# Key side of a four-layer kernel: gathers and projections paired across slots, copies ahead of maxima, exponentials two by two

## The chip, the cores and the metric

One core of one Trainium2 chip runs the whole program. The metric is the device time in microseconds (us) of one execution.

## What is computed

The reference adds four layers to `x` (32 batches of 64 rows by 512, float32), with a context tensor of the same shape: a cross-attention over 8 heads, a feed-forward with quantized weights, a linear cross-attention, and a projection with a low-rank mixture of experts. The change lies in the part that prepares the third layer from the context. Cut to that part, the reference is:

```python
kh = jnp.einsum('bcn,oc->bon', k, Wk).reshape(b, HEADS, DIM_HEAD, -1)   # k = v = ctx, n = 512
vh = jnp.einsum('bcn,oc->bon', v, Wv).reshape(b, HEADS, DIM_HEAD, -1)
kh = jax.nn.softmax(kh, axis=-1)
context = jnp.einsum('bhdn,bhen->bhde', kh, vh)
```

`context` is 64 by 64 for each head and batch. The kernel keeps, as `k.M`, that product already multiplied by the output weights `Wo`.

## The kernel before

`key_side` (from L214) is the first stage of the program. Behind it come `attention0`, `feed_forward`, `query_side` and `projection_and_experts`, and each stage ends in a meeting of all engines. The key side works on 16 tiles; tile t is two batches, 128 rows of the context. Each engine has its program written out by hand, as a loop over t and over four slots c of a tile, and semaphores join them. In slot (t, c) tile t is turned and gathered, while the next tile, t+1, is projected. These are the pieces, by the names of the helpers:

- `keys(t, c)` (L610, TensorE, "K"): one 128-wide chunk of the key projection, three float16 passes of two matmuls each, into `psK[c % 2]`. It waits until the exponentials of chunk c-2 have read that bank (`ek_ok`).
- `keys_max(t, c)` (L408, VectorE): the maximum over the row of `psK`, 1,024 wide, into `mk`.
- `exponentials(t, c)` (L553, ScalarE): two exponentials of 512 from `psK` into `ek`, each with its sum.
- `turn(t, j, b)` (L621, TensorE, "T"): four transposes of `ek` into `psT[b]`. ScalarE (L586, b = 0) or VectorE (`turned`, L413, b = 1, and b = 0 as well for j = 3) copies the bank to `eT`.
- `gather(t, j)` (L631, TensorE, "G"): `eT` times the turned context `cT`, summed over j = 0 to 3 in the single bank `psG`. Since the first gather of a tile starts a new sum there, it waits until the sum of the tile before has been copied away.
- That copy is the one to `gT` (L592, ScalarE), once a tile, in slot c = 0; `matrix(t)` (L644, TensorE, "M") multiplies `gT` by the weights in slot 2 of the tile after, and VectorE's `matrix` (L423) scales the result into `k.M`.
- `context(t)` (L602, TensorE, "C"): four transposes of the next context tile into `psM`, copied to `cT` by ScalarE (`transposed`, L548).

The two waits of a gather that the change touches stand in three lines:

```python
if j == 0:
    pe.wait_ge(cT_ok, t + 1)
    wait(pe, gT_ok, t)
```

Between these, VectorE also has sums of magnitudes of the feed-forward's weights (`magnitudes`, L429, slot 3 of tiles 0 to 4), row statistics (`stats`, L436, slots 0 and 3 of tiles 6 to 13) and, in the last tile, the reciprocal deviations (`vec_x`, from L98). ScalarE has two sums of magnitudes a tile in slots 2 and 3 of tiles 0 to 4, and one in tile 5. GpSimd casts the feed-forward's weights from tile 7 on (`ternary`, L366), behind `scales` (L469) on VectorE in slot 0 of tile 7.

Of the kernel before, what the change touches and what calls it, by code (L numbers as in the profile page):

```python
# [30 lines left out]
NC = L // P  # L31
BATCHES = 32
TILES = BATCHES * D // P
# [180 lines left out]
def key_side(nc, a, k):  # L214

    with ExitStack() as ctx:
# [41 lines left out]
        def sums_at(t):  # L258
            return range(3 * t, min(3 * t + 3, UNITS))
# [142 lines left out]
        def _(dve):  # L402
# [5 lines left out]
            def keys_max(t, c):  # L408
                dve.wait_ge(k_ps, NC * t + c + 1)
                wait(dve, ek_ok, 2 * NC * (t - 1) + 2 * c + 2)  # L410
                dve.tensor_reduce(mk[:, c, :], psK[c % 2][:, :, :], X, ALU.max, negate=True).then_inc(mk_ok, 1)  # L411

            def turned(t, j, b):  # L413
                dve.wait_ge(t_ps, 2 * NC * t + 2 * j + b + 1)
                wait(dve, g_ps, NC * (t - 1) + j + 1)
                dve.tensor_copy(eT[b][:, j, :], psT[b][:, :]).then_inc(eT_dve, 1)  # L416
# [97 lines left out]
            keys_max(1, 0)  # L514
            for t in range(TILES + 1):
                for c in range(NC):
                    if t + 1 + (c + 1) // NC < TILES:
                        keys_max(t + 1 + (c + 1) // NC, (c + 1) % NC)
                    if t < TILES:
                        if c == NC - 1:  # L520
                            turned(t, c, 0)
                        turned(t, c, 1)
                    if c == 0 and t < TILES:
                        sums(t)
                    if c == 0 and 1 <= t < 4:
                        biases(t - 1)
                    if c == 1 and t + 2 < TILES:
                        low(t + 2)
                    if c == 2 and t > 0:
                        matrix(t - 1)  # L530
                    if c == 3:
                        for u in sums_at(t):
                            if u % 3 == 2:
                                magnitudes(u)
                    if c == 0 and t == CAST - 1:
                        dve.wait_ge(wa_act, UNITS - UNITS // 3)
                        dve.wait_ge(wa_dve, UNITS // 3)
                        dve.tensor_reduce(asum[:, :], k.wabs[:, :, :], X, ALU.add).then_inc(sum_ok, 1)
                    if c == 0 and t == CAST:
                        scales()  # L540
                    if c in (0, 3) and STATS <= t < STATS + TILES // 2:
                        stats(2 * (t - STATS) + c // 3)
                    if c == 1 and t == TILES - 1:
                        vec_x(dve)

        @block.scalar
        def _(act):
# [33 lines left out]
            for t in range(TILES + 1):  # L581
                for c in range(NC):
                    if t < TILES and c < NC - 1:
                        act.wait_ge(t_ps, 2 * NC * t + 2 * c + 1)
                        wait(act, g_ps, NC * (t - 1) + c + 1)
                        act.activation(eT[0][:, c, :], psT[0][:, :], ACT.Copy).then_inc(eT_act, 1)  # L586
                    if t + 1 + (c + 1) // NC < TILES:
                        exponentials(t + 1 + (c + 1) // NC, (c + 1) % NC)
                    if c == 0 and t > 0:
                        act.wait_ge(g_ps, NC * t)  # L590
                        wait(act, m_ps, t - 1)
                        act.activation(gT[:, :], psG[:, :], ACT.Copy).then_inc(gT_ok, 1)  # L592
                    if c == 1 and t + 1 < TILES:
                        transposed(t + 1)
                    if c >= 2 and c - 2 < len(sums_at(t)):
                        magnitudes(sums_at(t)[c - 2])
                    if c == 1 and t == TILES - 1:
                        act_x(act)

        @block.tensor  # L600
        def _(pe):
# [97 lines left out]
            pe.wait_ge(w_ok, VO_OK)  # L699
            for t in range(TILES + 1):  # L700
                for c in range(NC):
                    if t + 1 + (c + 1) // NC < TILES:
                        keys(t + 1 + (c + 1) // NC, (c + 1) % NC)
                    if t < TILES:
                        turn(t, c, 0)
                        turn(t, c, 1)
                    if c > 0 and t < TILES:
                        gather(t, c - 1)
                    if c == 0 and t > 0:
                        gather(t - 1, NC - 1)  # L710
                    if c == 1 and t + 1 < TILES:
                        if t == CAST:
                            pe.wait_ge(inv_ok, 1)
                        context(t + 1)
                    if c == 2 and t > 0:
                        matrix(t - 1)
                    if c == 3 and t == CAST - 1:
                        pe.wait_ge(sum_ok, 1)
                        pe.wait_ge(M_ok, t)
                        pe.matmul(psM[:, 0:3], k.ones32[:, :], asum[:, :], start=True, stop=True).then_inc(sum_ps, 1)  # L720
# [1136 lines left out]
```

## Time and profile before

| | |
|---|---|
| median of 3 runs | 778.26 us (777.91 to 778.72) |
| the profiled execution | 775.0 us, its span 773.2 us |
| granted clock of TensorE, mean over the span | 0.96 of full speed |
| TensorE busy | 684.9 us, 89% |
| VectorE busy | 624.1 us, 81% |
| ScalarE busy | 487.6 us, 63% |
| GpSimd busy | 382.3 us, 49% |
| the key side | from 0 to about 221.6 us of the span |

The span runs from the first to the last instruction. The execution's own time is 1.8 us more. Shares of busy time are averages over five stages; only the first is changed. In a timeline the ends of matmuls are modelled, and one group of matmuls overlaps the next, so that the pace of TensorE is read from one start to the next start. An "idle before" is counted from a modelled end.

### The profile page before, as it was taken

The numbers are of one execution on the slowest core, as the hardware profiler recorded it, in microseconds if no ns is written. First come the engines' busy times: TensorE is split into PE (matmuls) and PEld (weight loads), VectorE is DVE, ScalarE is ACT, GpSimd is POOL, SyncE is SP. The second block draws the span as 40 slices with busy tenths as digits, with TensorE's granted clock in tenths as the row PEclk, the third lists the DMA queues.
The fourth block names the chain that finished last, engine by engine and source line by source line (L and its number), as shares of the span: only waits on it lengthen the run. The fifth ranks groups of instructions, "written<-read, shape, count | busy, mean of one in ns | idle before, by whom it ended". The sixth has DMA issues, their size and how long they took to land. (4 is left out here: it accounts for less than half of the span.)

```text
span 773.2 us, 17952 instructions
## 1 busy us (share of the span) xinstructions
PE 684.9 (89%) x6761; PEld 355.1 (46%) x6761; DVE 624.1 (81%) x1001; ACT 487.6 (63%) x896; POOL 382.3 (49%) x281
## 2 busy tenths in 40 slices
PE   4999999999977777399999859999999999938998
PEld 2455455554545555144444314444444444415743
DVE  6888788888636677589999658999999999939675
ACT  4878876767526667277766416878878788744320
POOL 2000029999915665021221127768677686728730
PEclk9999999999989999599999969999999999977999
DMA  6244546556352331033344300000000000007505
GB/s 166 80 136 163 172 151 178 147 128 169 79 136 72 79 86 32 14 59 60 70 77 78 57 0 1 1 2 1 1 2 1 1 2 1 1 1 117 104 27 191
DMA packets 94185, 54.93 MB, mean 71 GB/s; under 512 B 78548, under 2 KB 78548, under 8 KB 94100
## 3 DMA queue, kind: packets, MB, share of 16 engines
q1 hardware_dynamic: 93348, 53.25, 27.1%
q8 instruction: 55, 0.90, 0.5%
q10 hardware_dynamic: 752, 0.52, 0.3%
q14 instruction: 30, 0.25, 0.1%
HBM read 32.20 MB, written 4.19 MB: 47 GB/s over the span
## 5 line engine op out<-in xcount | busy, mean ns | idle before, releaser
L1312 POOL TENSOR_TENSOR query_qn<-query_eq,query_rq 128x1024 f32<-128x1024 f32 x64 | 121.7, 1902 | 56.9 <-DVE query_rq L1246 55.1
L558 ACT ACTIVATE keys_ek<-keys_psK,keys_mk 128x512 f32<-128x512 f32 x128 | 86.8, 683 | 38.4 <-DVE keys_mk L411 36.6
L411 DVE TENSOR_REDUCE keys_mk<-keys_psK 128x2 f32<-128x1024 f32 x64 | 77.8, 1217 | 17.1 <-PE keys_psK L617 16.9
L1237 DVE TENSOR_REDUCE query_mq<-query_psQ 128x16 bf16<-128x1024 f32 x64 | 75.6, 1181 | 5.3 <-PE query_psQ L1380 5.0
L1321 ACT ACTIVATE query_eq<-query_psQ 128x1024 f32<-128x1024 f32 x64 | 65.1, 1018 | 22.6 <-PE query_psQ L1393 22.6
L1243 DVE TENSOR_REDUCE query_lq<-query_eq 128x16 f32<-128x1024 f32 x64 | 77.2, 1207 | 2.6 <-ACT query_eq L1321 2.5
L1040 POOL TENSOR_SCALAR ff_hr<-ff_h,ff_qs 128x1376 f32<-128x1376 f32 x16 | 22.6, 1412 | 104.5 <-DVE ff_qs L1087 104.5
L1402 PE MATMUL query_psX<-all_ident,query_qn 128*128 128x128 f32 x512 | 70.7, 282 | 0.0
L628 PE MATMUL keys_psT<-all_ident,keys_ek 128*128 128x128 f32 x512 | 70.0, 280 | 0.0
L640 PE MATMUL keys_psG<-keys_eT,keys_cT 128*64 128x512 f32 x256 | 69.0, 617 | 1.0 <-issue 0.9
L628 PEld LDWEIGHTS keys_psT<-all_ident,keys_ek 128*128 128x128 f32 x512 | 54.8, 141 | 27.8 <-issue 20.0
L1328 ACT ACTIVATE query_qT<-query_psX 128x1024 f32<-128x1024 f32 x64 | 65.4, 1022 | 1.2 <-PE query_psX L1402 1.2
L1412 PE MATMUL query_psF<-query_qT,all_M 128*64 128x512 f32 x256 | 61.8, 604 | 1.1 <-ACT query_qT L1328 1.1
L1402 PEld LDWEIGHTS query_psX<-all_ident,query_qn 128*128 128x128 f32 x512 | 55.5, 142 | 15.7 <-issue 14.3
L376 POOL TENSOR_SCALAR keys_st<-all_ring 128x1024 bf16<-128x1024 f32 (+2 forms) x16 | 60.7, 3795 | 1.3
L364 POOL TENSOR_SCALAR keys_cs_hi<-all_cf 128x512 f16<-128x512 f32 x16 | 9.9, 618 | 95.5 <-DMA all_cf<-in_ctx_dram 87.0
L1161 PE MATMUL ff_psG<-all_wgT,ff_xT 128*128 128x512 bf16 (+1 forms) x192 | 46.8, 367 | 10.2 <-DMA ff_xT<-ff_xq 10.2
L416 DVE COPY keys_eT<-keys_psT 128x512 f32<-128x512 f32 x80 | 53.1, 680 | 2.4 <-PE keys_psT L628 2.3
L1134 ACT ACTIVATE ff_r<-ff_psG,all_sg 128x512 f32<-128x512 f32 (+1 forms) x48 | 30.8, 642 | 36.3 <-PE ff_psG L1161 34.7
L1166 PE MATMUL ff_psU<-all_wuT,ff_xT 128*128 128x512 bf16 (+1 forms) x192 | 46.1, 363 | 0.0
L1175 PE MATMUL ff_psD<-all_wdT,ff_hT 128*128 128x512 bf16 (+1 forms) x176 | 42.1, 390 | 4.4 <-DMA ff_hT<-ff_hq 4.4
L586 ACT ACTIVATE keys_eT<-keys_psT 128x512 f32<-128x512 f32 x48 | 28.7, 598 | 19.2 <-PE keys_psT L628 19.0
(255 smaller groups left out, 1481.9 us busy)
## 6 DMA issues: line engine op xcount, KB each, us to landing
all_ring<-in_L_ffn_w_down_dram SPq DMA_DIRECT2D x8, 688.0 KB, 4.3
all_ring<-in_L_ffn_w_gate_dram SPq DMA_DIRECT2D x10, 512.0 KB, 4.5
all_ring<-in_L_ffn_w_up_dram SPq DMA_DIRECT2D x10, 512.0 KB, 3.8
all_x_res<-in_x_dram SPq DMA_DIRECT2D x4, 1024.0 KB, 6.2
att_ctx_n<-in_ctx_dram SPq DMA_DIRECT2D x16, 256.0 KB, 3.0
out_dram<-all_x_res SPq DMA_DIRECT2D x16, 256.0 KB, 2.2
all_cf<-in_ctx_dram SPq DMA_DIRECT2D x15, 256.0 KB, 2.7
att_w_nat<-in_L_ffn_W_dram SPq DMA_DIRECT2D x4, 256.0 KB, 4.2
```

The source lines that it names most:

```text
L376: pool.tensor_scalar(st[v % 2][:, 0:w], r, -ROUND, 0.0, ALU.add, ALU.add).then_inc(cast_ok, 1)
L411: dve.tensor_reduce(mk[:, c, :], psK[c % 2][:, :, :], X, ALU.max, negate=True).then_inc(mk_ok, 1)
L558: act.activation(ek[t % 2][b][:, c, :], psK[c % 2][:, b, :], ACT.Exp, bias=mk[:, c, b:b + 1], accum_out=le[t % 2][:, b, c:c + 1]).then_inc ...
L628: mm = pe.transpose(chunk(psT[b], c), chunk(ek[t % 2][b][:, c, :], j), k.ident[:, :])
L640: mm = pe.matmul(psG[HALF[b], :], cT[t % 2][:, j, b * D:(b + 1) * D], eT[b][:, j, :], start=j == 0, stop=j == NC - 1)
L1237: dve.tensor_reduce(mq[g % 2][:, :, 0:HEADS], psQ[g % 2][:, :, :].rearrange("p b (h d) -> p b h d", d=D), X, ALU.max, negate=True).then_in ...
L1243: dve.tensor_reduce(lq[:, :], eq[g % 3][:, :, :], X, ALU.add).then_inc(lq_ok, 1)
L1312: pool.tensor_tensor(qn[m % 2][:, :, :], eq[m % 3][:, :, :], rq[m % 2][:, :].unsqueeze(2).broadcast_to([P, 2 * HEADS, D]), ALU.mult).then_ ...
L1321: act.activation(eq[g % 3][:, :, :].rearrange("p h d -> p (h d)"), psQ[g % 2][:, :, :].rearrange("p b n -> p (b n)"), ACT.Exp).then_inc(eq ...
L1328: act.activation(qT[t % 2][:, :, c * P:(c + 1) * P], psX[:, :, :].rearrange("p b (j n) -> p (b j) n", n=P), ACT.Copy).then_inc(qT_ok, 1)
L1402: mm = pe.transpose(psX[:, b, j * P:(j + 1) * P], qn[g % 2][:, b * HEADS + 2 * j:b * HEADS + 2 * j + 2, :].rearrange("p h d -> p (h d)"), ...
L1412: mm = pe.matmul(psF[HALF[b], :], k.M[:, 2 * t + b, j, :], qT[t % 2][:, b * NC + j, :], start=j == 0, stop=j == NC - 1)
```

## The change

On TensorE the pieces of every second slot (c = 1 and 3) are put in reverse. Slots 0 and 2 still run K, T, G; slots 1 and 3 now run G, T, K, so that the K of slot 1 stands beside the K of slot 2, and the G of slot 0 beside the G of slot 1. On VectorE the copies of a slot go ahead of its maximum. On ScalarE slots 0 and 2 have both pairs of exponentials, slots 1 and 3 none.

```diff
--- before.py
+++ after.py
@@ -514,12 +514,12 @@
             keys_max(1, 0)
             for t in range(TILES + 1):
                 for c in range(NC):
-                    if t + 1 + (c + 1) // NC < TILES:
-                        keys_max(t + 1 + (c + 1) // NC, (c + 1) % NC)
                     if t < TILES:
                         if c == NC - 1:
                             turned(t, c, 0)
                         turned(t, c, 1)
+                    if t + 1 + (c + 1) // NC < TILES:
+                        keys_max(t + 1 + (c + 1) // NC, (c + 1) % NC)
                     if c == 0 and t < TILES:
                         sums(t)
                     if c == 0 and 1 <= t < 4:
@@ -584,7 +584,9 @@
                         act.wait_ge(t_ps, 2 * NC * t + 2 * c + 1)
                         wait(act, g_ps, NC * (t - 1) + c + 1)
                         act.activation(eT[0][:, c, :], psT[0][:, :], ACT.Copy).then_inc(eT_act, 1)
-                    if t + 1 + (c + 1) // NC < TILES:
+                    if c % 2 == 0 and (t > 0 or c > 0) and t + (c + NC) // NC < TILES:
+                        exponentials(t + (c + NC) // NC, c)
+                    if c % 2 == 0 and t + 1 + (c + 1) // NC < TILES:
                         exponentials(t + 1 + (c + 1) // NC, (c + 1) % NC)
                     if c == 0 and t > 0:
                         act.wait_ge(g_ps, NC * t)
@@ -699,19 +701,23 @@
             pe.wait_ge(w_ok, VO_OK)
             for t in range(TILES + 1):
                 for c in range(NC):
-                    if t + 1 + (c + 1) // NC < TILES:
+                    if c % 2 == 1 and t < TILES:
+                        gather(t, c - 1)
+                    if c % 2 == 0 and t + 1 + (c + 1) // NC < TILES:
                         keys(t + 1 + (c + 1) // NC, (c + 1) % NC)
                     if t < TILES:
                         turn(t, c, 0)
                         turn(t, c, 1)
-                    if c > 0 and t < TILES:
-                        gather(t, c - 1)
-                    if c == 0 and t > 0:
-                        gather(t - 1, NC - 1)
                     if c == 1 and t + 1 < TILES:
                         if t == CAST:
                             pe.wait_ge(inv_ok, 1)
                         context(t + 1)
+                    if c % 2 == 1 and t + 1 + (c + 1) // NC < TILES:
+                        keys(t + 1 + (c + 1) // NC, (c + 1) % NC)
+                    if c == 2 and t < TILES:
+                        gather(t, c - 1)
+                    if c == 0 and t > 0:
+                        gather(t - 1, NC - 1)
                     if c == 2 and t > 0:
                         matrix(t - 1)
                     if c == 3 and t == CAST - 1:
```

The first place is TensorE at the start of a tile, tile 2 being turned and tile 3 projected. L617 is K, L628 is T, L640 is G, L607 is C; a last digit in a name is the number of a buffer. Before:

```order
L640 MATMUL keys_psG<-keys_eT0,keys_cT1 64x512 [waits keys_eT_dve]
L640 MATMUL keys_psG<-keys_eT1,keys_cT1 64x512
L617 MATMUL keys_psK0<-keys_cs_hi1,all_wk_hi 128x512 [waits keys_ek_ok,keys_lo_ok]
L617 MATMUL keys_psK0<-keys_cs_hi1,all_wk_hi 128x512
L617 MATMUL keys_psK0<-keys_cs_lo1,all_wk_hi 128x512 x2
L617 MATMUL keys_psK0<-keys_cs_hi1,all_wk_lo 128x512 x2
L628 MATMUL keys_psT0<-all_ident,keys_ek00 128x128 [waits keys_eT_act,keys_ek_ok]
L628 MATMUL keys_psT0<-all_ident,keys_ek00 128x128 x3
L628 MATMUL keys_psT1<-all_ident,keys_ek01 128x128 [waits keys_eT_dve,keys_ek_ok]
L628 MATMUL keys_psT1<-all_ident,keys_ek01 128x128 x3
L640 MATMUL keys_psG<-keys_eT0,keys_cT0 64x512 [waits keys_eT_act,keys_eT_dve,keys_gT_ok,keys_cT_ok]
L640 MATMUL keys_psG<-keys_eT1,keys_cT0 64x512
```

Now (two lines further down in the file, as L619, L630, L642 and L609):

```order
L630 MATMUL keys_psT1<-all_ident,keys_ek01 128x128 [waits keys_eT_dve,keys_ek_ok]
L630 MATMUL keys_psT1<-all_ident,keys_ek01 128x128 x3
L642 MATMUL keys_psG<-keys_eT0,keys_cT1 64x512 [waits keys_eT_dve]
L642 MATMUL keys_psG<-keys_eT1,keys_cT1 64x512
L642 MATMUL keys_psG<-keys_eT0,keys_cT0 64x512 [waits keys_eT_act,keys_eT_dve,keys_gT_ok,keys_cT_ok]
L642 MATMUL keys_psG<-keys_eT1,keys_cT0 64x512
L630 MATMUL keys_psT0<-all_ident,keys_ek00 128x128 [waits keys_eT_act,keys_ek_ok]
L630 MATMUL keys_psT0<-all_ident,keys_ek00 128x128 x3
L630 MATMUL keys_psT1<-all_ident,keys_ek01 128x128 [waits keys_eT_dve,keys_ek_ok]
L630 MATMUL keys_psT1<-all_ident,keys_ek01 128x128 x3
L609 MATMUL keys_psM<-all_ident,all_cf1 128x128 [waits keys_M_ok,keys_lo_ok]
L609 MATMUL keys_psM<-all_ident,all_cf1 128x128 x3
```

The two gathers into `psG` now stand one behind the other, the last of the tile before and the first of the new one, and the second of them has the wait on `gT_ok`. Before, a K and a T with a place of their own stood between them.

The second place is ScalarE in slots 0 and 1 of the same tile. L586 is the copy of a turned bank, L558 the exponentials, L592 (now L594) the copy to `gT`, L551 the copy of the turned context. Before:

```order
L586 ACTIVATE keys_eT0<-keys_psT0 128x512 [waits keys_g_ps,keys_t_ps]
L558 ACTIVATE keys_ek10,keys_le1<-keys_psK1,keys_mk 128x512 [waits keys_rl_ok,keys_t_ps,keys_mk_ok]
L558 ACTIVATE keys_ek11,keys_le1<-keys_psK1,keys_mk 128x512
L592 ACTIVATE keys_gT<-keys_psG 128x512 [waits keys_m_ps,keys_g_ps]
L586 ACTIVATE keys_eT0<-keys_psT0 128x512 [waits keys_g_ps,keys_t_ps]
L558 ACTIVATE keys_ek10,keys_le1<-keys_psK0,keys_mk 128x512 [waits keys_rl_ok,keys_t_ps,keys_mk_ok]
```

Now:

```order
L586 ACTIVATE keys_eT0<-keys_psT0 128x512 [waits keys_g_ps,keys_t_ps]
L558 ACTIVATE keys_ek10,keys_le1<-keys_psK0,keys_mk 128x512 [waits keys_rl_ok,keys_t_ps,keys_mk_ok]
L558 ACTIVATE keys_ek11,keys_le1<-keys_psK0,keys_mk 128x512
L558 ACTIVATE keys_ek10,keys_le1<-keys_psK1,keys_mk 128x512 [waits keys_rl_ok,keys_t_ps,keys_mk_ok]
L558 ACTIVATE keys_ek11,keys_le1<-keys_psK1,keys_mk 128x512
L594 ACTIVATE keys_gT<-keys_psG 128x512 [waits keys_m_ps,keys_g_ps]
L586 ACTIVATE keys_eT0<-keys_psT0 128x512 [waits keys_g_ps,keys_t_ps]
L551 ACTIVATE keys_cT1<-keys_psM 128x512 [waits keys_g_ps,keys_c_ps]
```

Two pairs of exponentials stand between the first copy and the copy to `gT`, where there was one.

The third place is VectorE between slot 3 of tile 2 and slot 0 of tile 3. L416 is a copy of a turned bank, L411 a maximum, L433 a sum of magnitudes. Before:

```order
L411 TENSOR_REDUCE keys_mk<-keys_psK0 128x2
L416 COPY keys_eT0<-keys_psT0 128x512
L416 COPY keys_eT1<-keys_psT1 128x512
L433 TENSOR_REDUCE all_wabs<-all_ring 128x1
L411 TENSOR_REDUCE keys_mk<-keys_psK1 128x2
L416 COPY keys_eT1<-keys_psT1 128x512
```

Now:

```order
L416 COPY keys_eT0<-keys_psT0 128x512
L416 COPY keys_eT1<-keys_psT1 128x512
L411 TENSOR_REDUCE keys_mk<-keys_psK0 128x2
L433 TENSOR_REDUCE all_wabs<-all_ring 128x1
L416 COPY keys_eT1<-keys_psT1 128x512
L411 TENSOR_REDUCE keys_mk<-keys_psK1 128x2
```

The copies of slot 3 moved ahead of its maximum, and so did the copy of slot 0.

## Rows read from the trace of the kernel before

**Rows 1.** the page's 40 slices of 19.3 us: busy tenths of TensorE, its granted clock

```profile
PE   4999999999977777399999859999999999938998
...
PEclk9999999999989999599999969999999999977999
```

**Rows 2.** timeline of TensorE, tiles 6 and 7: start, us from start to end, what ran

```profile
103.77 1.08 PE L640 MATMUL keys_psG<-keys_eT,keys_cT 128*64 128x512 f32 x4
104.68 1.04 PE L649 MATMUL keys_psM<-all_wv_wo,keys_gT 128*64 128x128 f32 x16
105.65 0.39 PE L617 MATMUL keys_psK<-keys_cs_hi,all_wk_hi 64*128 64x512 f16 x2
105.88 0.38 PE L617 MATMUL keys_psK<-keys_cs_lo,all_wk_hi 64*128 64x512 f16 x2
...
106.41 1.09 PE L628 MATMUL keys_psT<-all_ident,keys_ek 128*128 128x128 f32 x8
107.43 1.08 PE L640 MATMUL keys_psG<-keys_eT,keys_cT 128*64 128x512 f32 x4
108.44 0.39 PE L720 MATMUL keys_psM<-keys_asum,all_ones 128*128 128x3 f32 x2
...
114.33 0.66 PE L607 MATMUL keys_psM<-all_ident,all_cf 128*128 128x128 f32 x4
114.91 0.39 PE L617 MATMUL keys_psK<-keys_cs_hi,all_wk_hi 64*128 64x512 f16 x2
```

**Rows 3.** TensorE's gathers: their group on the page, timeline at two late ones

```profile
L640 PE MATMUL keys_psG<-keys_eT,keys_cT 128*64 128x512 f32 x256 | 69.0, 617 | 1.0 <-issue 0.9
...
60.66 1.09 PE L628 MATMUL keys_psT<-all_ident,keys_ek 128*128 128x128 f32 x8
61.95 1.08 PE L640 MATMUL keys_psG<-keys_eT,keys_cT 128*64 128x512 f32 x4 [0.19 <-issue]
...
87.79 1.08 PE L640 MATMUL keys_psG<-keys_eT,keys_cT 128*64 128x512 f32 x4 [0.56 <-issue]
```

**Rows 4.** timeline of ScalarE ahead of those gathers, and after one maximum

```profile
59.92 0.69 ACT L558 ACTIVATE keys_ek<-keys_psK,keys_mk 128x512 f32<-128x512 f32 x1 [0.48 <-DVE keys_mk L411]
...
61.26 0.59 ACT L592 ACTIVATE keys_gT<-keys_psG 128x512 f32<-128x512 f32 x1
...
87.10 0.59 ACT L592 ACTIVATE keys_gT<-keys_psG 128x512 f32<-128x512 f32 x1
...
107.78 0.69 ACT L558 ACTIVATE keys_ek<-keys_psK,keys_mk 128x512 f32<-128x512 f32 x1 [2.21 <-DVE keys_mk L411]
```

**Rows 5.** timeline of VectorE, tiles 6 and 7

```profile
106.52 1.22 DVE L411 TENSOR_REDUCE keys_mk<-keys_psK 128x2 f32<-128x1024 f32 x1
107.66 1.28 DVE L416 COPY keys_eT<-keys_psT 128x512 f32<-128x512 f32 x2
108.85 0.68 DVE L440 BATCH_NORM_STATS2 keys_six<-all_x_res 128x6 f32<-128x512 f32 x1
...
109.67 1.21 DVE L411 TENSOR_REDUCE keys_mk<-keys_psK 128x2 f32<-128x1024 f32 x1
```

**Rows 6.** groups by line, 20 to 215 us: VectorE's five magnitudes (busy, mean ns)

```profile
L433 DVE TENSOR_REDUCE all_wabs<-all_ring 128x1 f32<-128x1024 f32 (+2 forms) x5 | 5.3, 1068 | 0.0
```

**Rows 7.** timeline of VectorE in the last tile of the key side

```profile
212.02 0.69 DVE L416 COPY keys_eT<-keys_psT 128x512 f32<-128x512 f32 x1 [1.23 <-PE keys_psT L628]
...
215.31 0.69 DVE L416 COPY keys_eT<-keys_psT 128x512 f32<-128x512 f32 x1
```

**Rows 8.** TensorE by stretch: us, PE busy, ..., granted clock before the DMA share

```profile
239.90:242.00 2.10, 0.05 (x1) 0.00 (x0) 0.73 (x2) 0.93 (x1) 1.25 (x2) 1.00 0.03 6
...
436.10:438.80 2.70, 0.04 (x1) 0.00 (x0) 2.56 (x8) 0.00 (x0) 1.33 (x1) 1.00 0.71 134
438.80:442.20 3.40, 3.02 (x8) 1.09 (x9) 0.18 (x1) 1.44 (x1) 0.08 (x1) 0.50 0.19 38
```

**Rows 9.** timeline of GpSimd: its last cast on the key side

```profile
209.07 4.84 POOL L376 TENSOR_SCALAR keys_st<-all_ring 128x1376 bf16<-128x1376 f32 x1
```

## The prediction

> **What bounds the kernel now.** I read the page's slices first. TensorE is busy without a break in the first eleven slices, at the full clock [rows 1]; that is the key side, the only stage that changes. Then the timeline of TensorE. From start to start, T takes 1.02 us (106.41 to 107.43), G 1.01 (to 108.44), or 0.91 where M follows it, M 0.97, K 0.76, C 0.58 [rows 2]. A tile is four times K, T and G, with one G at 0.91, and M and C: 3.04 + 4.08 + 3.94 + 0.97 + 0.58 = 12.6 us, with nothing waited for. So 16 tiles are about 200 of the 221.6 us of the stage: TensorE is the bound, and both what it saves and what it waits for shows in full.
>
> **What switching costs.** G is 0.10 shorter before M than before a matmul of another shape. G and M use the array as 128x64, T and C as 128x128, K as 64x128; so 0.10 us goes by when the shape changes. C has four transposes and T eight, so that one is (1.02 - 0.58) / 4 = 0.11, and T's remaining 0.14 is 0.10 for the way out and 0.04 for the way in. For G's way in I take the same 0.05. K loses about 0.08 on its way out: the first pass takes 0.23, three would be 0.68. The Trainium skill, in TensorEngine Tiling (Array Packing), section Key Properties, says that changing the tiling mode drains TensorE. The trace agrees, with the 0.10 us.
>
> **The change on TensorE.** Nothing is added or removed; only places move. The new order by slot, without waits:
> - slot 0: K after K 0.75, T 1.02, G before G 0.91: 2.68
> - slot 1: G after G 0.96, T before C 0.93, C 0.53, K before K 0.68: 3.10
> - slot 2: K 0.75, T 1.02, G before M 0.91, M 0.87: 3.55
> - slot 3: G after M 0.96, T 1.02, K before K 0.68: 2.66
>
> That is 12.0 us, 0.6 less than 12.6. If that were all, 15 tiles would save 9 us.
>
> **The wait that it meets.** The gather of slot 1 is the first of its tile. It writes `psG`, and must wait for the copy to `gT`. The trace has this wait already: the copy starts at 61.26 and takes 0.59, and the gather, 0.27 later than its T allows (1.29 behind it, not 1.02), starts at 61.95; the other ends at 87.69, and its gather starts at 87.79 [rows 3, 4]. So a gather starts 0.10 after that copy's end. In all they lost about 1.2 us before: 0.9 of modelled idle time [rows 3], and some 0.1 at each of three. Now this gather stands directly behind the last gather of the tile before, and the copy behind two pairs of exponentials on ScalarE. From the start of slot 0 (its K) the chain is:
> - T starts at 0.75 and ends 1.09 later, 1.84.
> - VectorE's copy starts at 1.88, and its next instruction 0.60 later (two copies in 1.19 [rows 5]), at 2.48. This is the maximum of slot 0's K, which now stands behind the copy. It takes 1.22, to 3.70.
> - The exponentials start 0.04 after a maximum (106.52 + 1.22, then 107.78 [rows 4, 5]), at 3.74. From the first of a pair to the copy to `gT` are 1.34 us (59.92 to 61.26). The copy runs from 5.08 to 5.67.
> - The gather starts at 5.77. TensorE was ready at 2.68: it stands for 3.09 us. After standing, this G takes 1.01 and not 0.96.
>
> A tile takes 12.0 + 3.09 + 0.05 = 15.1, or 2.5 us more than 12.6. It holds for tiles 1 to 14, which turn and project: **+35 us**. Queued behind the gather are the T of slot 1, C and two K, and with them every maximum and exponential of the next tile. Their work is done in the remaining 9.3 us of a tile with time to spare. By the same sums the last pair of exponentials of a tile ends at about 14.1, before slot 0 of the next starts at 15.1 with the K that needs its bank.
>
> **What makes the chain longer.** VectorE takes the maximum of the K before slot 0 at about 0.20, which holds it for 1.14 (106.52 to 107.66), to 1.35; then come statistics (0.82, 108.85 to 109.67 [rows 5]) or magnitudes, and then the copy, which could start at 1.88. The statistics of slot 3 end at 2.17, so the copy starts 0.29 late: 8 tiles, +2.3. Five magnitudes take 1.07 on the mean [rows 6], 0.08 less from start to start, and 0.53 of each is free: +2.3. Taken off are the 1.2 us lost before. ScalarE's magnitudes cost nothing: from its last pair to its next copy it has 2.4 us (14.1 to 16.5), and two of them, each at most two exponentials of 0.69 long, take no more than 2.8; the 0.4 over falls ahead of exponentials that wait for VectorE anyway. Without that cover they would cost up to 1 us in each of five tiles.
>
> **Edges.** In tile 0 there is no copy to wait for, and its first gather waits for a copy of ScalarE about as long as K does now: 0. In the last tile the copy of slot 2 stands 3.29 behind that of slot 1, with the row deviations between [rows 7]. The third gather waits for it, and T, two copies and the last gather now come behind that gather: T and a copy, 1.02 + 0.6, are no longer hidden. The first gather waits 0.9 for the copy to `gT` (0.17 of G's tail, 0.04, 0.59, 0.10). So +2.5, between 0 and 4.
>
> Together 35 + 2.3 + 2.3 - 1.2 + 2.5 = +41 us with the clock as it is.
>
> **The clock.** TensorE now stands still 14 times, for about 2.9 us by modelled ends, 3.2 with statistics and up to 3.9 with magnitudes. Before, a stretch of 2.10 us with 0.05 busy passed at the full 2.4 GHz, and after one of 2.70 with 0.04 busy the granted clock was 0.50, 1.2 GHz, for 3.4 us [rows 8]. The new ones are longer than both. At half the clock TensorE does half the work, and for 9.3 us after each wait it alone sets the pace: a fall costs up to 3.4 / 2 = 1.7 us, 1.6 on the mean, since the end of the wait may lie in it. How many are followed by a fall no row tells: the bounds are 0 and 14, 0 and +24 us. I take 11, nearer to the row of 2.70, since all of them are longer; but one case is little to go by: **+17 us**.
>
> GpSimd's casts end at 213.91 [rows 9], 7.7 us before the stage. They move back with the `scales` of tile 7 by less than the stage's end does, so they bind nothing.
>
> **The sum.** The profiled execution took 775.0; 775.0 + 41 + 17 = 833. The median of the runs is 3.3 us above it, so I forecast 836.
>
> **Rivals.**
> - *The clock holds.* The wait is there, but no fall follows. For it: 2.10 us passed without one. Against it: the row of 2.70. Time 778 + 41 = 819. Chance 0.17.
> - *Falls are worse.* One after each wait, with a second stretch at 1.2 GHz after some, or TensorE still slow in slot 0, where the chain to the copy begins: 35 us or more for the clock, 855. Chance 0.08.
> - *Fewer switches win.* By the rule of the Trainium skill named above this kernel would be faster, since five of thirteen changes of shape in a tile go. As a mechanism of this kernel: 0.6 us saved in each tile, if the gather of slot 1 finds `psG` free. It decides at a wait of 0.6 us a tile; the copy would have to end by 3.2 of the tile's time. That gives 9 us, 769, or a little less, since GpSimd's casts would move up by only 7 x 0.6, to 209.7, with a transfer behind them, and might end the stage: 770. Against it: even with ScalarE idle, the last gather ends at 2.85, and the copy and its two handovers (0.04 + 0.59 + 0.10) bring 3.6. Chance 0.04.
> - *The change doesn't do what it says.* The order of the instructions shows both gathers side by side, and the copy behind two pairs. Chance 0.01, at 778.
>
> **How the numbers follow.** My case has 0.70. Its range is 41 with 3 either way, and 8 to 14 falls: 829 to 845. For 8 in 10 the range takes in the clock that holds and part of the worse case: 817 to 847. About 0.2%, 1.6 us, is what a measurement of this kernel can tell from no change. Faster 0.04, same 0.01, slower 0.95.
>
> **What would show it.** In the profile after: gathers with 2.9 to 3.9 us idle before them in 14 tiles, starting 0.10 after a copy to `gT`; tiles of 15.1 us where the clock holds and about 16.7 where it falls; TensorE's busy share in the first twelve slices no longer 9; K to K and G to G without the 0.10. The rest of the kernel takes as long as before. I am wrong if the gather of slot 1 follows at once, if another wait in the tile is longer (a K that waits for exponentials), or if the granted clock in that stage stays at full.

## The result, and the profile after

The changed kernel takes 840.07 us (median of 4 runs, 839.74 to 843.95) against 778.12 (777.91 to 778.72) before: a ratio of 1.081, 95% interval 1.077 to 1.084. The profiled execution took 839.88, span 838.1, mean granted clock 0.941; before they were 775.0, 773.2 and 0.960.

First the page of the changed kernel: busy tenths of TensorE in 40 slices of 21 us, its granted clock, and the gathers' group (busy, mean ns, idle before them and who ended it).

```profile
PE   4788878886888677665999984999999999975998
...
PEclk9989998999999999996999997899999999996999
...
L642 PE MATMUL keys_psG<-keys_eT,keys_cT 128*64 128x512 f32 x256 | 70.1, 625 | 47.6 <-ACT keys_gT L594 45.8
```

The stage ends in slice 14 now, and none of its slices is a 9 [rows 1]. The idle time before the gathers went from 1.0 us to 47.6 [rows 3], 45.8 of it ended by ScalarE's copy to `gT`. Up to the first matmul of the attention the kernel took 221.96 us before and takes 285.10 now: 63.1 of the 64.9 us by which the span grew are in this stage, the other 1.7 in all the rest.

TensorE's timeline, tiles 12 and 13 (start, us from start to end, engine, line, operation, what it made from what, count; idle time before in brackets). The first row is a K; the K rows between are left out but for the ones that show a K behind a K.

```profile
220.49 0.38 PE L619 MATMUL keys_psK<-keys_cs_hi,all_wk_hi 64*128 64x512 f16 x2
...
221.23 1.09 PE L630 MATMUL keys_psT<-all_ident,keys_ek 128*128 128x128 f32 x8
222.25 1.08 PE L642 MATMUL keys_psG<-keys_eT,keys_cT 128*64 128x512 f32 x4
226.53 1.08 PE L642 MATMUL keys_psG<-keys_eT,keys_cT 128*64 128x512 f32 x4 [3.19 <-ACT keys_gT L594]
227.53 1.09 PE L630 MATMUL keys_psT<-all_ident,keys_ek 128*128 128x128 f32 x8
228.46 0.60 PE L609 MATMUL keys_psM<-all_ident,all_cf 128*128 128x128 f32 x4
229.00 0.39 PE L619 MATMUL keys_psK<-keys_cs_hi,all_wk_hi 64*128 64x512 f16 x2
...
229.65 0.38 PE L619 MATMUL keys_psK<-keys_cs_hi,all_wk_hi 64*128 64x512 f16 x2
...
230.40 1.09 PE L630 MATMUL keys_psT<-all_ident,keys_ek 128*128 128x128 f32 x8
231.42 1.08 PE L642 MATMUL keys_psG<-keys_eT,keys_cT 128*64 128x512 f32 x4
232.32 1.04 PE L651 MATMUL keys_psM<-all_wv_wo,keys_gT 128*64 128x128 f32 x16
...
241.88 1.98 PE L642 MATMUL keys_psG<-keys_eT,keys_cT 128*64 128x512 f32 x4 [3.19 <-ACT keys_gT L594]
```

Slot 0 is the K at 220.49, T and G. The G at 226.53 is the first gather of the next tile, in slot 1, and TensorE stands still 3.19 us before it. From it to the same gather one tile on, 241.88, are 15.35 us [rows 2 give 12.6 before]. K to K takes 0.65 (229.00 to 229.65), and G to M 0.90 (231.42 to 232.32).

VectorE and ScalarE over the same wait:

```profile
220.71 1.21 DVE L411 TENSOR_REDUCE keys_mk<-keys_psK 128x2 f32<-128x1024 f32 x1
221.84 0.69 DVE L440 BATCH_NORM_STATS2 keys_six<-all_x_res 128x6 f32<-128x512 f32 x1
...
222.66 0.67 DVE L416 COPY keys_eT<-keys_psT 128x512 f32<-128x512 f32 x1
223.25 1.21 DVE L411 TENSOR_REDUCE keys_mk<-keys_psK 128x2 f32<-128x1024 f32 x1
```

```profile
224.49 0.69 ACT L558 ACTIVATE keys_ek<-keys_psK,keys_mk 128x512 f32<-128x512 f32 x1 [0.63 <-DVE keys_mk L411]
...
225.83 0.59 ACT L594 ACTIVATE keys_gT<-keys_psG 128x512 f32<-128x512 f32 x1
```

From the K of slot 0 at 220.49 the chain reads: copy at 2.17, maximum 2.76 to 3.97, exponentials at 4.00, copy to `gT` 5.34 to 5.93, gather at 6.04. The statistics (from 221.84; the rest of them is left out) are what moved the copy from 1.88 to 2.17. In all 14 tiles the gather starts 0.10 after that copy's end.

Last, stretches of the same kernel (us, busy time and count of PE, PEld, DVE, ACT, POOL, the granted clock, DMA share, GB/s):

```profile
209.60:226.50 16.90, 13.73 (x92) 7.46 (x93) 10.77 (x16) 8.44 (x21) 13.14 (x8) 0.90 0.43 101
226.50:241.70 15.20, 12.16 (x92) 6.64 (x92) 10.71 (x16) 8.36 (x21) 9.61 (x6) 1.00 0.50 138
241.80:245.10 3.30, 3.22 (x10) 1.64 (x11) 0.00 (x0) 0.16 (x1) 3.22 (x2) 0.50 1.04 248
245.20:258.70 13.50, 10.39 (x83) 5.66 (x81) 9.97 (x14) 8.18 (x21) 13.25 (x6) 1.00 0.28 58
```

After the wait that ends at 241.88 the granted clock is 0.50 for 3.4 us, that is 1.2 GHz and not 2.4. After the wait that ends at 226.53, just as long, it stays at 1.00. So the same work has a price with and without a fall in one trace: 15.35 us for the tile from 226.53, and 16.99 for the one before it, whose gather starts at 209.54. A fall there costs 1.64; between other pairs of such gathers it costs 1.62 to 1.64, and 1.56 in the tile from 241.88. Such stretches at 0.50 follow 13 of the 14 waits.

### The profile page after: what moved, and what is told of

It reads as the page before. It is cut to its first block and busy times, and to the rows that moved or that the text cites. A ratio compares the mean times of both kernels' runs of the same rounds, so it can differ in the third digit from the quotient of the medians.

```text
span 838.1 us, 17925 instructions
## 1 busy us (share of the span) xinstructions
PE 694.9 (83%) x6734; PEld 370.4 (44%) x6761; DVE 624.7 (75%) x1001; ACT 487.6 (58%) x896; POOL 382.8 (46%) x281
## 5 line engine op out<-in xcount | busy, mean ns | idle before, releaser
L416 DVE COPY keys_eT<-keys_psT 128x512 f32<-128x512 f32 x80 | 53.5, 685 | 78.0 <-PE keys_psT L630 77.9
L642 PE MATMUL keys_psG<-keys_eT,keys_cT 128*64 128x512 f32 x256 | 70.1, 625 | 47.6 <-ACT keys_gT L594 45.8
L558 ACT ACTIVATE keys_ek<-keys_psK,keys_mk 128x512 f32<-128x512 f32 x128 | 86.6, 683 | 24.4 <-DVE keys_mk L411 24.3
L411 DVE TENSOR_REDUCE keys_mk<-keys_psK 128x2 f32<-128x1024 f32 x64 | 77.9, 1217 | 18.2 <-PE keys_psK L619 18.1
L630 PEld LDWEIGHTS keys_psT<-all_ident,keys_ek 128*128 128x128 f32 x512 | 62.7, 155 | 42.3 <-issue 39.8
L630 PE MATMUL keys_psT<-all_ident,keys_ek 128*128 128x128 f32 x512 | 79.9, 305 | 0.8 <-DVE keys_eT L416 0.4
L586 ACT ACTIVATE keys_eT<-keys_psT 128x512 f32<-128x512 f32 x48 | 28.6, 596 | 80.9 <-PE keys_psT L630 80.6
```

The costliest lines, as they stand in the source:

```text
L558: act.activation(ek[t % 2][b][:, c, :], psK[c % 2][:, b, :], ACT.Exp, bias=mk[:, c, b:b + 1], accum_out=le[t % 2][:, b, c:c + 1]).then_inc ...
L630: mm = pe.transpose(chunk(psT[b], c), chunk(ek[t % 2][b][:, c, :], j), k.ident[:, :])
L642: mm = pe.matmul(psG[HALF[b], :], cT[t % 2][:, j, b * D:(b + 1) * D], eT[b][:, j, :], start=j == 0, stop=j == NC - 1)
```

## The experiments

No kernel here leaves anything out. Ratios are to the kernel before on the same chip. The theory to test: the time is lost because the gather of slot 1 waits for the copy to `gT`, which stands behind VectorE's copy and maximum and ScalarE's pairs, and because the clock falls after that wait. The main rivals: the new orders on VectorE and ScalarE alone do the harm; or the harm is the wait alone and the clock only a by-product.

**Which engine's order does it.** Two kernels split the change. The first has its order on TensorE, and VectorE's and ScalarE's old ones:

```diff
 (VectorE, each slot)
+  if t + 1 + (c + 1) // NC < TILES: keys_max(...)    # back ahead of the copies
   turned(...)
-  if t + 1 + (c + 1) // NC < TILES: keys_max(...)
 (ScalarE, each slot)
-  if c % 2 == 0 and (t > 0 or c > 0) and t + (c + NC) // NC < TILES: exponentials(t + (c + NC) // NC, c)
-  if c % 2 == 0 and t + 1 + (c + 1) // NC < TILES: exponentials(...)
+  if t + 1 + (c + 1) // NC < TILES: exponentials(...)
```

> TensorE's new order alone, with VectorE and ScalarE in the order of before. My theory: the two gathers side by side are what costs, since the copy to gT lies between them whatever ScalarE does, so this is about as slow as the whole change. By the chain: the maximum of slot 0's K now stands behind the maximum and the two copies of slot 3 (0.20 + 1.14 + 1.19 = 2.53, against 2.48 in the change), so the gather of slot 1 starts at about 5.8 us of the tile again, and statistics and magnitudes on VectorE (0.82, 1.07) come on top in full. Part of the wait moves to the gather of slot 0, which waits 0.9 us for VectorE's copies; so fewer waits are long enough for the clock to fall. 827 us with the clock held, 848 with a fall in every tile; 838 between. Rival (the pairing of the exponentials ahead of the copy to gT is what costs): near the time of before, 780 us or less.

The second is its complement: only those two pieces of the change, with TensorE's old order.

> VectorE's and ScalarE's new order alone, with TensorE in the order of before. My theory: the copy to gT ends at 5.67 us of the tile as in the change, but the gather that waits for it has a K and a T ahead of it and is due at 4.56; so a tile loses 5.77 - 4.56 = 1.2 us and not 3.1, in part already at the K of slot 1, which waits for the first pair of exponentials. 14 x 1.2 = 17, 4.6 for statistics and magnitudes, less the 1.2 of before: 798 us, and the granted clock stays at full on the key side, as no wait is longer than 1.5 us. Rival (the pairing costs by itself all of the change's loss): 819 us or more. Rival (the order of VectorE and ScalarE is free): 778.

Measured: TensorE's order alone 849.09 us, ratio 1.093 (1.089 to 1.098); the other two alone 794.74, ratio 1.023 (1.019 to 1.026). TensorE's timeline in each, first TensorE's order alone, then the other two:

```profile
156.68 1.22 PE L628 MATMUL keys_psT<-all_ident,keys_ek 128*128 128x128 f32 x8 [1.36 <-DVE keys_eT L416]
...
161.14 1.08 PE L640 MATMUL keys_psG<-keys_eT,keys_cT 128*64 128x512 f32 x4 [2.22 <-ACT keys_gT L592]
...
168.06 0.63 PE L628 MATMUL keys_psT<-all_ident,keys_ek 128*128 128x128 f32 x4 [0.77 <-DVE keys_eT L416]
```

```profile
147.97 0.39 PE L619 MATMUL keys_psK<-keys_cs_hi,all_wk_hi 64*128 64x512 f16 x2 [0.67 <-ACT keys_ek L558]
...
150.22 1.08 PE L642 MATMUL keys_psG<-keys_eT,keys_cT 128*64 128x512 f32 x4 [0.40 <-issue]
```

With the reversed order on TensorE alone the gather still waits, 2.22 us here, so the order of TensorE makes that wait; the two others only lengthen it, to 2.9 and more. The T of slot 0 now waits too, 1.36, for VectorE's copy, since the maximum of a K that ran just before is taken ahead of it, and the second half of slot 2's T waits 0.77. A tile takes about 17.0 where the clock holds; the one from 156.68, of which the rows are, takes 18.96, since the clock fell at 162.3. The complement has neither: the K of slot 1 waits 0.67 for exponentials that ScalarE takes a slot later, and a gather comes 0.40 late; its tile takes 13.8. So both rivals of an engine alone fall: TensorE's order costs the most, and the two others, which cost 17 us by themselves, take 9 off beside it. That the first took 849 and not the 838 I expected is VectorE's doing: T waits for its copies twice a tile. The clock fell four times on the key side, each time after a gather's wait of 2.22, and not after the longest one of 2.91.

VectorE's old order with everything else of the change completes the picture (edit: the first hunk above alone).

> The change without its VectorE part (maxima ahead of copies, as before). My theory: that part helps the new order of TensorE. Without it T of slot 0 waits 1.36 us, and the copy to gT starts at about 6.1 us of the tile, so its gather starts at 6.8 and not 5.77; another 0.8 us goes at the T of slot 2: 14 x 1.8 = 25 us. But each wait at the gather is shorter, since part of it went before, about 2.3 us, so that fewer falls of the clock follow, 15 us less: about 850 us. Rival (VectorE's part causes the wait, as its copy stands ahead of the maximum that the chain needs): 820 or less.

It took 845.73, ratio 1.088 (1.085 to 1.091):

```profile
156.33 1.23 PE L630 MATMUL keys_psT<-all_ident,keys_ek 128*128 128x128 f32 x8 [1.36 <-DVE keys_eT L416]
...
160.85 1.08 PE L642 MATMUL keys_psG<-keys_eT,keys_cT 128*64 128x512 f32 x4 [2.29 <-ACT keys_gT L594]
...
166.16 0.63 PE L630 MATMUL keys_psT<-all_ident,keys_ek 128*128 128x128 f32 x4 [0.78 <-DVE keys_eT L416]
```

Three waits, 4.4 us a tile together, the longest 2.29; the tile takes 17.0. In the early tiles with magnitudes the gather waits up to 2.91. The granted clock is 1.00 from 20 to 265.2 us and falls once on the key side, for 3.4 us, behind the wait of 2.29 that ends at 263.90. This kernel has more idle time than the changed one and is only 6 us slower, since it keeps its clock in all tiles but that one.

**What the copy to `gT` stands behind.** In slot 0 that copy goes ahead of both pairs of exponentials; nothing else of the change is touched.

```diff
 (ScalarE, slot c of tile t)
+  if c == 0 and t > 0:                       # waits g_ps, copies psG to gT
+      ...
   if c % 2 == 0 and (t > 0 or c > 0) ...: exponentials(...)
   if c % 2 == 0 and t + 1 ...: exponentials(...)
-  if c == 0 and t > 0:
-      ...
```

> The whole change, but on ScalarE the copy to gT of slot 0 goes ahead of both pairs of exponentials. My theory: the copy then runs from 2.89 (the last gather's end at 2.85 and 0.04) to 3.48, and the next gather starts at 3.58 where TensorE was ready at 2.68: a wait of 0.9 us and not 3.1. Tile 12.0 + 0.9 + 0.05 = 12.95, 0.35 more than before; 14 x 0.35 = 5, 2.5 in the last tile, less 1.2: 784 us, and no fall of the clock from these waits. Rival (the wait isn't the copy but the copies of the turned banks, or VectorE's maxima): it stays above 820 us.

Measured: 788.31, ratio 1.014 (1.010 to 1.018), 52 us less than the changed kernel. ScalarE and TensorE at one such gather:

```profile
140.96 0.60 ACT L590 ACTIVATE keys_gT<-keys_psG 128x512 f32<-128x512 f32 x1 [0.86 <-PE keys_psG L642]
```

```profile
139.84 1.08 PE L642 MATMUL keys_psG<-keys_eT,keys_cT 128*64 128x512 f32 x4
141.66 1.08 PE L642 MATMUL keys_psG<-keys_eT,keys_cT 128*64 128x512 f32 x4 [0.74 <-ACT keys_gT L590]
```

The wait is 0.74 instead of 3.19, and a tile takes 12.91 (the next gather starts at 154.57). 0.74 is what is left when ScalarE stands ready: the handover, the copy of 0.60 and 0.10 more. So 2.45 of the 3.19 us (of the tiles with statistics) are the exponentials ahead of the copy and the maximum that they wait for. With two gathers side by side the wait cannot go below 0.74 here, while the saved changes of shape give 0.6.

From gather to gather its tiles are 0.24 longer on the mean than the kernel before's, 3 of the 10 us by which this one is slower than 778. Some 4 more come from one tile. TensorE, VectorE and GpSimd there:

```profile
202.77 1.98 PE L642 MATMUL keys_psG<-keys_eT,keys_cT 128*64 128x512 f32 x4 [2.64 <-DVE keys_eT L416]
```

```profile
197.76 4.26 DVE L406 TENSOR_TENSOR keys_cs_lo<-all_cf,keys_cs_hi 128x512 f16<-128x512 f32 x1
201.95 0.68 DVE L416 COPY keys_eT<-keys_psT 128x512 f32<-128x512 f32 x1
```

```profile
197.55 4.84 POOL L376 TENSOR_SCALAR keys_st<-all_ring 128x1376 bf16<-128x1376 f32 x1
```

VectorE's subtraction for `cs_lo` began 0.21 us after a cast of GpSimd and took 4.26 us, where it takes 0.68 in most other tiles; the copy behind it came late, the gather waited 2.64, and ran at half the clock, which fell behind this wait, for 3.4 us. That chance meeting of VectorE and GpSimd is seen again below.

**The clock.** Does a fall cost what I put down, or would TensorE have been idle anyway? This kernel keeps the wait but puts ten bf16 matmuls of 128x512 into it, which write a bank that is free and whose result nobody reads:

```diff
 (TensorE, ahead of slot 1's gather, tiles 1 to 15)
+  if c == 1 and 0 < t < TILES:
+      pe.wait_ge(cT_ok, t + 1)
+      wait(pe, M_ok, t - 1)
+      if t == CAST:
+          pe.wait_ge(inv_ok, 1)
+      for _ in range(10):
+          pe.matmul(psM[:, :], k.ident16[:, :], k.ind[:, :], start=True, stop=True)
```

> The whole change, with ten bfloat16 matmuls of 128x512 on constants added between the two gathers of tiles 1 to 15, into the bank psM, which is free there (2.2 us of TensorE, in a wait of 2.9 to 3.9 us; nothing reads their result). My theory: the waits stay, so that nothing of the 41 us is won back, but TensorE isn't idle through them, and the granted clock stays at full: 840 less 13 falls of 1.6 us, 819 us. Rival (the falls are not from the waits, or they cost nothing because a tile is bound by other engines): 840 us. If some waits with magnitudes or statistics still leave over 1 us idle and fall, between the two.

Measured: 821.5, ratio 1.056 (1.052 to 1.060). TensorE at one wait, and the stretch it lies in:

```profile
180.83 1.08 PE L643 MATMUL keys_psG<-keys_eT,keys_cT 128*64 128x512 f32 x4 [0.93 <-issue]
...
192.93 2.33 PE L711 MATMUL keys_psM<-all_ind,all_ident 128*128 128x512 bf16 x10
196.18 1.08 PE L643 MATMUL keys_psG<-keys_eT,keys_cT 128*64 128x512 f32 x4 [0.92 <-issue]
```

```profile
176.00:191.00 15.00, 14.07 (x101) 7.20 (x100) 10.36 (x17) 8.44 (x21) 12.01 (x8) 1.00 0.51 119
```

A tile takes 15.35 (180.83 to 196.18), to the hundredth what the changed kernel takes where its clock holds, so in such a tile the filler changed nothing but the falls: the granted clock is 1.00 in every stretch from 29.6 to 265. Against the changed kernel that is 18.6 us. Thirteen falls at 1.63 are 21.2, and the stage, up to the first matmul of the attention, is 16.95 shorter in the two traces (268.15 against 285.10). Two things account for most of the difference. The first late gather starts 2.34 later (41.76 against 39.42), behind a stretch at 0.50 from 19.4 to 29.6 us, where the changed kernel has 3.4 us of it. And in tile 15, where the wait is only 0.74, the filler holds up the gather: 3.27 us from the gather before it (252.55 to 255.82) against 1.82 (270.74 to 272.56). More work made the kernel faster.

**Keeping the saving without the wait.** The order of the slots is mended: the gather of slot 1 goes to slot 1's end, slot 3 keeps it first, and the copy to `gT` stands between the two pairs.

```diff
 (ScalarE)
   if c % 2 == 0 and (t > 0 or c > 0) ...: exponentials(t + (c + NC) // NC, c)
-  if c % 2 == 0 and t + 1 + (c + 1) // NC < TILES: exponentials(...)
   if c == 0 and t > 0: ...                   # the copy to gT
+  if c % 2 == 0 and t + 1 + (c + 1) // NC < TILES: exponentials(...)
 (TensorE)
-  if c % 2 == 1 and t < TILES: gather(t, c - 1)
+  if c == 3 and t < TILES - 1: gather(t, c - 1)
   ...                                        # T, then context(t + 1)
+  if c == 1 and t < TILES or c == 3 and t == TILES - 1: gather(t, c - 1)
```

> A version meant to keep what the change saves and avoid its wait. Slot 1 of TensorE runs T, C, G, K (the gather behind the turned context), slot 3 G, T, K as in the change but for the last tile, which keeps the order of before; on ScalarE the copy to gT stands between the two pairs of exponentials of slot 0. By the rows of before: slot 0 2.78, slot 1 1.46 + 1.01 + 0.68 = 3.15, slot 2 3.55, slot 3 2.66: 12.14 us a tile, 0.46 less than 12.6. The copy to gT ends at about 4.03 and the gather is due at 4.24, so nothing waits in a plain tile. 14 x 0.46 = 6.4, and the 1.2 us that gathers lost before: 7 to 8 us faster than before, a ratio of 0.990, if statistics and magnitudes find room. Rival (the copy is late here too, or the second pair of exponentials holds up the K of slot 2): each 0.5 us of wait in a tile takes all of it back, ratio 1.00. Rival (changes of shape cost nothing, the 0.10 us was something else): 1.00 with no wait seen.

Measured: 774.37, ratio 0.995 (0.993 to 0.997); timed again on the chip of two further kernels, with the expectation

> The kernel e5_gather_late again, beside the other two on the same chip, so that the 2 us between it and e8_late_dev can be told: ratio to before 0.995.

773.45, ratio 0.996 (0.994 to 0.997). A tile takes 12.22 with no wait in it (from one K behind a K to the same K a tile on), 0.4 less than the 12.6 of before, so of the 0.6 us that fewer changes of shape were to give, 0.4 arrive: this order keeps one more change. Fifteen such tiles are 6 us, and 4 came, half of the 7 to 8 expected. The rest of the 6 went in the last tile, in two waits of 1.99 and 0.45 us. The two K first, then TensorE, VectorE, ScalarE and GpSimd in the last tile:

```profile
137.93 0.38 PE L619 MATMUL keys_psK<-keys_cs_hi,all_wk_hi 64*128 64x512 f16 x2
...
150.15 0.38 PE L619 MATMUL keys_psK<-keys_cs_hi,all_wk_hi 64*128 64x512 f16 x2
```

```profile
210.68 1.04 PE L651 MATMUL keys_psM<-all_wv_wo,keys_gT 128*64 128x128 f32 x16
213.72 0.63 PE L630 MATMUL keys_psT<-all_ident,keys_ek 128*128 128x128 f32 x4 [1.99 <-ACT keys_eT L586]
```

```profile
207.85 0.69 DVE L416 COPY keys_eT<-keys_psT 128x512 f32<-128x512 f32 x1 [1.23 <-PE keys_psT L630]
208.46 4.13 DVE L98 TENSOR_SCALAR all_rs_v<-all_mv 128x16 f32<-128x16 f32 x1
```

```profile
212.63 0.21 ACT L111 ACTIVATE all_rs_ln<-all_rs_v 128x16 f32<-128x16 f32 x1 [4.62 <-DVE all_rs_v L98]
...
213.00 0.58 ACT L586 ACTIVATE keys_eT<-keys_psT 128x512 f32<-128x512 f32 x1
```

```profile
207.72 4.84 POOL L376 TENSOR_SCALAR keys_st<-all_ring 128x1376 bf16<-128x1376 f32 x1
```

T waits for a bank that ScalarE has not copied yet (its copy starts at 213.00). That copy stands behind ScalarE's part of the row deviations, which waits for VectorE's; and VectorE's first instruction of them, 128x16 in SBUF, took 4.13 us. It ends at 212.59, and GpSimd's cast of 4.84 ends at 212.56. In the kernel before the same instruction took 1.32 and ended at 213.94, with the last cast ending at 213.91 [rows 9]. In the changed kernel it runs with GpSimd idle, and took 0.16. So it stands until the cast is over, as the subtraction above nearly did: that one ended at 202.02, and its cast at 202.39. The Trainium skill, SBUF — State Buffer, section Terms, has the rule for it: VectorE and GpSimd share a pair of ports that is held for the full instruction, and the loser blocks fully. The trace agrees in the time of the end, to 0.03 us, for the instruction of the row deviations; the subtraction ended 0.37 before its cast. That the ports are the cause no run here shows, and not every cast had this effect: in the kernel with the copy ahead the same subtraction took its usual 0.68 from 133.23, wholly within a cast from 131.42 to 135.05. What decides is open. VectorE's copy at 207.85, which reads PSUM, took 0.69 beside that cast, as everywhere.

Then the row deviations were moved behind the last copies, on VectorE and ScalarE, in this kernel and alone in the kernel before:

```diff
 (VectorE)
-  if c == 1 and t == TILES - 1: vec_x(dve)
+  if c == 0 and t == TILES: vec_x(dve)
 (ScalarE)
+  if c == 0 and t == TILES: act_x(act)
   if c == 0 and t > 0: ...                   # the copy to gT
-  if c == 1 and t == TILES - 1: act_x(act)
```

> The kernel e5_gather_late, with the row deviations of the last tile (VectorE's and ScalarE's, slot 1) moved behind the last copies. In e5_gather_late VectorE's first instruction of them took 4.13 us, from 208.46 to 212.59, where GpSimd's last cast ends at 212.56; ScalarE's copy waited behind it, and T of slot 2 lost 1.99 + 0.45 us. My theory: moved, this wait is gone and nothing else waits for the deviations before the stage's end; the stage ends about 2.2 us earlier: ratio to before 0.992 where e5_gather_late had 0.9949. Rival (the stage's end is set by GpSimd's casts and their transfers, whose last queue entry was at 216.1 us): it gains less than 1 us.

> The kernel before, with the same move of the row deviations alone. There the first instruction took 1.32 us and nothing on TensorE waited for it by more than 0.1 us, so my theory gives no change: ratio 1.000, within 0.001. Rival (moving them is a gain by itself): 2 us faster, 0.997.

Measured: in the mended order 770.46, ratio 0.991 (0.990 to 0.993); in the kernel before 777.26, ratio 1.001 (0.999 to 1.002). TensorE in the mended one, last tile:

```profile
208.56 1.04 PE L651 MATMUL keys_psM<-all_wv_wo,keys_gT 128*64 128x128 f32 x16
209.54 1.09 PE L630 MATMUL keys_psT<-all_ident,keys_ek 128*128 128x128 f32 x8
210.56 2.18 PE L642 MATMUL keys_psG<-keys_eT,keys_cT 128*64 128x512 f32 x8
```

T now follows M at once. The move gains 3.0 us over the mended order timed beside it (773.45), more than the 2.2 expected; in the trace of that one the clock also fell once behind its wait, at 213.6. Where TensorE did not wait for the deviations, in the kernel before, the same move is worth nothing. This version is 0.9% faster than the kernel before and 8.3% faster than the changed one.

**VectorE's order in the mended kernel.** The maxima go back ahead of the copies there, to see whether VectorE's part of the change is needed.

> The kernel e5_gather_late, with VectorE's maxima ahead of its copies again, as before the change. My theory: the K at the end of slot 3 and the T of slot 0 stand side by side on TensorE, and that T needs the bank that VectorE's copies of slot 3 free; behind the maximum they come about 1.4 us late, as in the run with TensorE's order alone. So each of 15 tiles loses 1.4 us or more: 770 + 21 or more, 791 to 800 us. Rival (VectorE's part of the change does nothing): as e5_gather_late.

Measured: 817.29, ratio 1.050 (1.048 to 1.053), worse than I expected by 17 us and more.

```profile
142.56 1.23 PE L630 MATMUL keys_psT<-all_ident,keys_ek 128*128 128x128 f32 x8 [1.36 <-DVE keys_eT L416]
...
145.69 0.63 PE L630 MATMUL keys_psT<-all_ident,keys_ek 128*128 128x128 f32 x4 [0.31 <-DVE keys_eT L416]
...
150.53 0.63 PE L630 MATMUL keys_psT<-all_ident,keys_ek 128*128 128x128 f32 x4 [0.78 <-DVE keys_eT L416]
```

```profile
157.86 1.22 PE L630 MATMUL keys_psT<-all_ident,keys_ek 128*128 128x128 f32 x8 [1.36 <-DVE keys_eT L416]
```

A tile takes 15.30 (142.56 to 157.86), 3.1 more than 12.22, and 14 of them are the 43 us. K stands in pairs between the T now, and each maximum of 1.22 lies ahead of a copy that the next T needs: three waits of 1.36, 0.31 and 0.78, more than I had priced, and halves of T that run apart. So with slots reversed on TensorE, VectorE's copies must go first. That part of the change is not what hurt.

## Why the prediction was right, and where it was off

The forecast was 836 us, 817 to 847, slower; measured 840.07.

- **The wait.** Predicted: a gather at 5.77 after the start of slot 0, 6.06 behind statistics; the trace has 6.04. Standing still 2.9, 3.2 and up to 3.9 us was foreseen, and the 14 waits are 2.92 to 3.88. A tile without a fall takes 15.35, against 15.1 and 0.29. One of the eight waits behind statistics, that of tile 7, was 2.92 and not 3.2. The step that carries the result, reading the length of a chain on three engines from the trace of another order, held to a few hundredths.
- **The fewer changes of shape.** K to K without the change came as worked out (0.65 against 0.68), and so did G behind M (0.96, 233.20 to 234.16). G to G can't be seen here, since the second always waits. The mended kernel shows that the saving is real where nothing waits, and it is small.
- **The terms without the clock.** +41 predicted. From the first late gather (39.42) to the fourteenth (258.79) there are 13 tiles, 54.3 us longer than before; 12 of the falls lie in them, 19.6 us, so that 34.7 are left, 2.67 a tile. (The prediction counts tiles of 12.6; the kernel before averages 12.7 with the late gathers, which is its term of -1.2.) The prediction's 35, 2.3, 2.3 and -1.2 come to 38.4 over 14 tiles, 2.74 a tile. The whole stage is 63.1 longer; less 13 falls at 1.63 that is 41.9.
- **The magnitudes of ScalarE** were costed at nothing, and no wait in the 14 tiles goes beyond what VectorE's account for.
- **The last tile**: +2.5 predicted; from its first T to its last gather it takes 11.3 us (269.58 to 280.88) against 9.1 before, +2.2. Its first gather waits 0.74, not 0.9.
- **The clock**: the mechanism was right, the size not quite. I took 11 falls at 1.6, +17 us. There were 13 after the 14 waits, at 1.63, 21 us, and one more of 3.4 us at 19.9, in slot 0 of tile 0, where the kernel before kept 1.00. That one is hardly the change's: the kernel before with only its row deviations moved, all of it far behind this point, has such a fall at 20.7. This term was mis-sized by 4 us or more. It was the one with the least behind it, one stretch of 2.70 us in the trace of before [rows 8].
- **A loose reading.** TensorE was said to be busy without a break in the first eleven slices. The first of them is a 4 [rows 1]: the time before the loop, which is as long in both kernels. Nothing rests on it.
- **The rest of the kernel** was to take as long as before, and took 1.7 more in the trace. That is within what this part varies by from one profiled execution to the next: over the twelve traces, whose code behind the key side is the same, it took 550.3 to 554.5 us, and 554.5 and 551.5 in two of one kernel, the mended order.
- Some luck is in the 4 us by which the forecast was off. The conversion to a median added 3.3 us because the profiled execution before lay that much under it. The one after lies at its median, so that against 833 the profiled 839.88 is off by 7, and the addition hid 3 of it.

Of the rivals, "the clock holds" fell with the granted clock of the profile after, and the filler shows what it would have been: 821.5, where 819 was worked out. "Fewer switches win" did not come about, and the kernel with the copy ahead shows why: even with ScalarE ready 0.74 us remain, against its point of 0.6. "Falls are worse" did not come about either: each fall lasted 3.4 us, and slot 0 of tiles 1 to 15 was never inside one.

Two expectations about experiments missed widely, by 11 us and by 17 or more, and both on VectorE's old order. Each time T waited for VectorE's copies at more places of the tile than I had worked out. The mended order came to 0.995 and not 0.990, mainly since the last tile's waits were not foreseen. Four others were 2.5 to 4.3 us off: 794.74 for 798, 788.31 for 784, 821.5 for 819 and 845.73 for 850.

## What to carry to other kernels

Before two uses of one bank are put side by side to save a change of the array's shape, work out the chain that empties the bank from start to start, with what is queued ahead of the emptying copy on its engine: here 0.6 us were to be saved and 3.1 were paid, in every tile. A wait of TensorE in a loop can be paid twice, as idle time and as a slower clock behind it; three shorter waits (4.4 us a tile together, the gather's mostly 2.2 to 2.3) brought one fall in one kernel and four in another, where a single one of about 3.2 a tile brought 13. When an order on one engine is turned around, look at which of the queues behind it need turning too, and at the small instructions among them, since one late copy there holds TensorE.

## What the hardware showed

- A VectorE instruction of 0.16 us on 128x16 in SBUF took 1.32 and 4.13 us, and both times ended 0.03 us after a GpSimd cast that was under way when it began; another, with two inputs in SBUF, took 4.26 in place of 0.68, but 0.68 wholly within another cast. Copies from PSUM beside such casts took their usual 0.69.
- The clock fell after 13 of 14 waits of 2.9 to 3.9 us, in a loop that is otherwise full of work, and not after the one that ended at 226.53, as long as its neighbours. With several shorter waits in a tile, most of them under 2.3 us and up to 2.9 beside magnitudes, one kernel had one fall on the key side and another four, all behind waits of 2.2 to 2.3 and none behind the one of 2.9. In a third kernel the clock fell behind a wait of 2.64, the only long one there. So the length of the last wait alone does not decide; what does is open.
- Ten matmuls that compute nothing, put into each wait, made the kernel 2.2% faster (840.07 to 821.5).
